# Layer 3 of a four-layer graph network: the edge products of a step at other places of a written-out order

## The chip, the cores and the metric

The kernel runs on one core of a Trainium2 chip. The metric is the time of one execution in microseconds (us), taken on the device. Three executions of the kernel before were timed, and a fourth was recorded by the hardware profiler.

## The reference, cut to what matters

Four graph layers work on 6250 nodes with 128 features and 100,000 edges sorted by destination. The change touches the fourth, "layer 3", alone: ten steps of a propagation (APPNP) over the graph with a self loop at every node.

```python
# K = 10, ALPHA = 0.1; src, dst with self loops added; norm = deg^-1/2[src] * deg^-1/2[dst]
def step(xk, _):
    msg = norm[:, None] * xk[src]
    agg = jax.ops.segment_sum(msg, dst, num_segments=n_nodes)
    return ((1.0 - ALPHA) * agg + ALPHA * h, None)
xK, _ = jax.lax.scan(step, x, None, length=K)
return jax.nn.relu(xK)
```

Each step needs all rows of the result of the step before: every node sums over the rows of its sources, which lie anywhere.

## The kernel before, in words

The 6250 nodes are 49 tiles of 128 (`NT`). The state `y` of a step is kept in SBUF as two float16 halves, in A in one step and in E in the next. A step makes the sums of the 49 destination tiles in two ways.

**Dense part.** The destination tiles 0 to 38 (`DENSE`) are multiplied with the adjacency matrix, which lies in DRAM as fp8 counts. Four tiles are a chunk; there are ten, 0 to 9, and chunk 9 has three tiles. A chunk takes 49 entries, one for each source tile, of two matmuls (the halves) with 512 columns, in chunk 9 with 384 columns (line 1988). The matrix comes in three pieces for each chunk, into a ring of four (line 764, SyncE's queue); a piece is loaded anew as soon as TensorE has used the one in its place, that is after the entries 16, 32 and 48 of a chunk.

**Edge part.** For the destination tiles 39 to 48 the rows of `y` are gathered by edge: 162 tiles of 128 edges, in 41 groups (0 to 40) of four tiles, the last of two. GpSimd issues one indirect DMA for each tile (line 1034) from the copy of `y` in DRAM (`table` in even steps, `x_spill` in odd ones), into a ring of five groups in the tile `arena`; TensorE multiplies them with one-hot matrices (line 2017), which VectorE makes (line 2874). The sums come out as three more chunks, numbers 10, 11 and 12, of four, four and two tiles (39 to 42, 43 to 46, 47 and 48), finished after the groups 17, 33 and 40.

**Chunk to state.** A finished chunk is copied out of PSUM by ScalarE ("copy", line 1476), transposed by TensorE ("turn", line 2001), and scaled and added by VectorE (line 2853 makes the part that doesn't depend on the sums, line 2888 adds). ScalarE makes the upper halves (line 1460) and VectorE the lower ones (line 2863). Then SyncE stores the chunk's rows to DRAM ("store", line 792). GpSimd begins the gathers of the next step when all 13 stores of this step have landed.

**Order.** The order of all this on TensorE, VectorE, ScalarE and SyncE is a list, `plan`, sorted by a place in units (lines 384 to 401). One dense entry of four tiles takes 2 units, one of three tiles 1.5; a step is 955 units long (`LONG`), and the dense entries of the next step follow at once. Every engine takes the entries in this order and waits at each on semaphores. Group g of the edge products stands at `first + EDGE_GAP * g`; the turn of a chunk 10 units behind its end (`TURN_LAG`) and its store 26 units behind (`STORE_LAG`). In the kernel before, the groups of a step stand at 84 + 22 g, so group 40 at 964, nine units into the next step; in the first step at 115 + 22 g. The order at a step's end is: chunk 9 ends (955), group 40 and chunk 12 end (964), turn 9 (965), turn 12 (974), store 9 (981), the load of a piece behind entry 16 of the next step (987), store 12 (990).

**Waits of the next step.** A dense entry of chunk 0 reads the source tile of its number from the new state. Before the entries that are keys of `READ_UPTO` TensorE waits until the lower halves of all tiles below the value are there:

```python
READ_UPTO = {0: 32, 32: 36, 36: NT - 1, NT - 1: NT}                       # line 413
if n > 0 and what == 0 and i in READ_UPTO:                                  # line 1985
    pe.wait_ge(sem("lower"), max(NT + tiles_done(step - 1, j) for j in range(READ_UPTO[i])))
```

Of the kernel before, what the change touches and what calls it, by code (L numbers as in the profile page):

```python
# [17 lines left out]
NT = (N_NODES + P - 1) // P  # L18
# [24 lines left out]
DENSE = NT - POOLED  # L43
# [2 lines left out]
ADJ_PITCH = 1 << 13  # L46
CHUNKS = (DENSE + CHUNK - 1) // CHUNK
POOL_CHUNKS = (POOLED + CHUNK - 1) // CHUNK
TURN_LAG, STORE_LAG, EDGE_LAG, EDGE_LATE, EDGE_GAP = 10, 26, 84, 115, 22
SCALE = 1024.0  # L50

BD, BK = 5, 26
# [37 lines left out]
def build(nc, t, out):  # L90
    ctx = ExitStack()
    with ctx:
# [23 lines left out]
        def sem(name):  # L116
            name = one_branch.get(name, name)
            if name not in names:
                names[name] = ctx.enter_context(nc.semaphore(name))
            return names[name]  # L120
# [227 lines left out]
        def chunk_nodes(c):  # L348
            if c < CHUNKS:
                return range(c * CHUNK, min((c + 1) * CHUNK, DENSE))  # L350
            return range(DENSE + (c - CHUNKS) * CHUNK, min(DENSE + (c - CHUNKS + 1) * CHUNK, NT))

        def chunk_at_cost(c):
            return 2 * NT * min(c * CHUNK, DENSE) // CHUNK
# [18 lines left out]
        def pooled_group(c):  # L373
            return (pooled_last[c - CHUNKS] - edge_first) // EG
# [10 lines left out]
        for step in range(STEPS):  # L385
            base = step * LONG
            for c in range(CHUNKS):
                for i in range(NT):
                    plan.append((base + chunk_at_cost(c) + 2 * i * len(chunk_nodes(c)) / CHUNK, 0, "dense", step, c, i))
                plan.append((base + chunk_at_cost(c + 1), -1, "copy", step, c, 0))  # L390
                plan.append((base + chunk_at_cost(c + 1) + TURN_LAG, 1, "turn", step, c, 0))
                plan.append((base + chunk_at_cost(c + 1) + STORE_LAG, 4, "store", step, c * CHUNK, chunk_nodes(c).stop))
            first = base + (EDGE_LAG if step else EDGE_LATE)
            for g in range(EGROUPS):
                plan.append((first + EDGE_GAP * g, 2, "edges", step, g, 0))
                plan.append((first + EDGE_GAP * g - 5 * EDGE_GAP // 2, 5, "hots", step, g, 0))
            for c in range(CHUNKS, CHUNKS + POOL_CHUNKS):
                plan.append((first + EDGE_GAP * pooled_group(c), 3, "copy", step, c, 0))
                plan.append((first + EDGE_GAP * pooled_group(c) + TURN_LAG, 1, "turn", step, c, 0))
                plan.append((first + EDGE_GAP * pooled_group(c) + STORE_LAG, 4, "store", step, chunk_nodes(c).start, chunk_nodes(c).stop))  # L400
# [9 lines left out]
        def tiles_done(step, i):  # L410
            return place[step, i] + 1

        READ_UPTO = {0: 32, 32: 36, 36: NT - 1, NT - 1: NT}

        assert edge_first >= 600
        taken, edges_in, done0, done_in = 0, {}, [], {}
# [62 lines left out]
        first = [("first", r) for r in range(PTN)]  # L479
# [1077 lines left out]
        def _(pe):  # L1557
# [363 lines left out]
            def after_l2(b):  # L1921
# [46 lines left out]
                if b == 0:  # L1968
# [4 lines left out]
                    for kind, step, what, i in plan:  # L1973
                        n = step * CHUNKS + what
                        if kind == "dense":
# [7 lines left out]
                            if n == 0 and i % T7 == 0:  # L1983
                                pe.wait_ge(sem("y_lower0"), i // T7 + 1)
                            if n > 0 and what == 0 and i in READ_UPTO:
                                pe.wait_ge(sem("lower"), max(NT + tiles_done(step - 1, j) for j in range(READ_UPTO[i])))
                            for h in range(2):
# [1095 lines left out]
```

## Time and profile before

| | us |
|---|---|
| median of 3 runs | 4969.4 (4966.07 to 4975.6) |
| the profiled execution's own time | 4971.43 |
| its span, from the first to the last instruction | 4969.5 |
| first and last dense matmul of layer 3 | 2686.7 and 4957.7 |
| mean granted TensorE clock | 0.915 |

The profile is one execution. Times are from the start of its span. For each group of instructions it has the busy time and the idle time of the engine before it, with what ended that idle time. "PE" is TensorE's matmul, "PEld" its weight load, "DVE" VectorE, "ACT" ScalarE, "POOL" GpSimd; "SPq" is SyncE's issue of a DMA. L1034 is line 1034 of the kernel.

Columns of the views: waits have who waited for whom, the total in us, the times and the longest. Windows have the stretch and its length, the busy us and count of PE, PEld, DVE, ACT and POOL, the granted TensorE clock as a share of full speed, the busy share of the DMA engines and GB/s; a step is taken from its first dense matmul to that of the next. A timeline has start, duration, the instruction, how many are merged (x), and in brackets the idle time before with what ended it. The chain has start, duration and what.

### The profile page before, as it was taken

To read this page: it belongs to the slowest core of one execution; us is meant where nothing else is said; L and a number is where in the kernel's file an instruction comes from. 1 tells how busy PE (TensorE), PEld (TensorE's weight loads), DVE (VectorE), ACT (ScalarE), POOL (GpSimd) and SP (SyncE) were. 2 spreads that over 40 slices of the span, in tenths; PEclk is the share of its full clock that TensorE was granted. 3 is DMA by queue.
4 is the path that set the end of the run, shared out by engine and by line. 5 is a ranking of instruction groups with operands and counts; after the bars stand their busy time and mean duration, and the time that the engine had idled before them with its cause. 6 is when DMAs were issued, how large, how long until landed. Compare 5 with 4: busy or idle time off the path is not lost.

```text
span 4969.5 us, 72321 instructions
## 1 busy us (share of the span) xinstructions
PE 4197.7 (84%) x25760; PEld 2695.7 (54%) x25760; DVE 2560.9 (52%) x8838; ACT 1034.5 (21%) x2922; POOL 3260.7 (66%) x3390
## 2 busy tenths in 40 slices
PE   3999588999985555667667999999999999999999
PEld 2776466766664555556554444444544444444444
DVE  7999545565554677778796222232232323222323
ACT  5887411111111001112224000000000000000101
POOL 2552377777775777777751767676766767676766
PEclk9999789999997667778778999999999999999999
DMA  5332322222222333333333666666666666666665
GB/s 150 113 111 97 86 66 70 71 66 70 71 70 70 94 96 95 96 95 95 88 78 105 204 190 204 198 202 201 205 199 199 204 196 208 196 203 198 202 200 165
DMA packets 455501, 686.46 MB, mean 138 GB/s; under 512 B 91793, under 2 KB 237879, under 8 KB 455120
## 3 DMA queue, kind: packets, MB, share of 16 engines
q1 hardware_dynamic: 341188, 454.71, 29.2%
q0 software_dynamic: 107584, 223.83, 17.2%
q8 instruction: 210, 3.44, 0.3%
q10 hardware_dynamic: 6364, 3.20, 0.2%
q14 instruction: 155, 1.27, 0.1%
HBM read 599.50 MB, written 82.31 MB: 137 GB/s over the span
## 4 chain that ended last, share of the span: by engine, by line
PE 31%; POOL 12%; DVE 6%; issue 5%; DMA 4%; ACT 1%; SPq 0%; POOLq 0%; DVEq 0%
PE ps L1988 26%; POOL arena L1034 10%; POOL E L999 2%; DVE B L2517 1%; DMA arena<-x_spill,src_i 1%; PE pt L2017 1%; DMA arena<-table,src_i 1%; PE ps L1810 1%; PE ps L2001 1%; PE pt L1827 1%; PE pt L1818 1%; DVE arena L2559 1%; DMA x_spill<-A 1%; DMA table<-E 0%; PE ps L1937 0%
## 5 line engine op out<-in xcount | busy, mean ns | idle before, releaser
L1988 PE MATMUL ps<-arena,E 128*128 128x512 fp8e4 (+1 forms) x4900 | 1080.6, 375 | 8.3 <-DVE C L2786 7.0
L1034 POOL DMA_INDIRECT arena<-table,src_i x810 | 782.0, 965 | 458.5 <-issue 233.6
L1988 PE MATMUL ps<-arena,A 128*128 128x512 fp8e4 (+1 forms) x4900 | 1078.9, 374 | 0.0
L1034 POOL DMA_INDIRECT arena<-x_spill,src_i x810 | 780.4, 963 | 348.6 <-issue 235.4
L984 POOL DMA_INDIRECT arena<-table,src_i x782 | 743.3, 950 | 346.9 <-issue 236.1
L999 POOL DMA_INDIRECT E<-gat_table,src_i x782 | 763.6, 976 | 269.8 <-issue 234.2
L1733 PE MATMUL ps<-E,arena 128*128 128x352 f32 (+22 forms) x2932 | 737.1, 403 | 118.4 <-DMA arena<-table,src_i 110.2
L1988 PEld LDWEIGHTS ps<-arena,E 128*128 128x128 f16 x4900 | 465.0, 98 | 507.3 <-issue 8.5
L1988 PEld LDWEIGHTS ps<-arena,A 128*128 128x128 f16 x4900 | 464.4, 98 | 495.7 <-issue 5.5
L2888 DVE SCALAR_TENSOR_TENSOR C<-ps,sc_b,scores 128x128 f32<-128x128 f32 x490 | 138.8, 345 | 1090.6 <-PE ps L2001 1089.0
L1733 PEld LDWEIGHTS ps<-E,arena 128*128 128x128 f32 x2932 | 491.2, 201 | 291.5 <-DMA arena<-table,src_i 141.0
L2437 DVE SCALAR_TENSOR_TENSOR E<-arena,pt 128x512 f32<-128x512 bf16 (+5 forms) x782 | 479.0, 675 | 24.5 <-PE ps L1733 23.7
L1810 PE MATMUL ps<-arena,B 128*128 128x144 f32 x2244 | 477.9, 364 | 0.0
L1810 PEld LDWEIGHTS ps<-arena,B 128*128 128x128 f32 x2244 | 391.4, 240 | 8.1 <-issue 5.9
L1476 ACT ACTIVATE O<-ps 128x512 f32<-128x512 f32 x100 | 58.7, 587 | 1527.9 <-PE ps L1988 1527.9
L1858 PE MATMUL pt<-ident,E 128*128 128x128 f32 x56 | 25.4, 454 | 354.6 <-ACT E L1268 354.6
L1069 POOL DMA_INDIRECT A<-first_rows,src_i x162 | 171.3, 1057 | 221.3 <-PE pt L2056 124.1
L1543 ACT ACTIVATE E<-ps 128x490 fp8e4<-128x490 f32 (+1 forms) x507 | 299.8, 596 | 61.6 <-PE ps L2072 57.6
L2081 PE MATMUL pt<-arena,E 128*128 128x258 f16 x1911 | 296.3, 275 | 1.4 <-ACT E L1543 1.3
L2874 DVE TENSOR_SCALAR rows<-w_gat,dst_f 128x54 f16<-128x54 bf16 (+17 forms) x966 | 159.3, 256 | 254.5 <-PE pt L2017 236.8
L2517 DVE TENSOR_SCALAR B<-w_gat,dst_f 128x256 f32<-128x256 bf16 x784 | 244.5, 381 | 0.0
L3002 DVE TENSOR_SCALAR O<-arena 128x245 bf16<-128x245 bf16 x1014 | 233.1, 293 | 4.1 <-PE ps L2072 4.0
(350 smaller groups left out, 4424.9 us busy)
## 6 DMA issues: line engine op xcount, KB each, us to landing
arena<-adj SPq DMA_DIRECT2D x180, 1024.0 KB
arena<-adj SPq DMA_DIRECT2D x90, 1088.0 KB
adj<-E SPq DMA_DIRECT2D x39, 784.0 KB, 3.7
arena<-table,src_i POOLq DMA_INDIRECT x1592
O<-dst_rows SPq DMA_DIRECT2D x112, 224.0 KB
arena<-adj SPq DMA_DIRECT2D x20, 768.0 KB
x_spill<-A SPq DMA_DIRECT2D x55, 256.0 KB, 2.5
arena<-x_spill,src_i POOLq DMA_INDIRECT x810
```

Source lines behind the costliest of these rows:

```text
L984: pool.indirect_dma_start(out=rows_ring[:, k % RING, :], out_offset=None, in_=table, in_offset=bass.IndirectOffsetOnAxis(ap=src_i[:, k:k + ...
L999: pool.indirect_dma_start(out=att_rows[:, b % 3 * AB + at, :], out_offset=None, in_=gat_table, in_offset=bass.IndirectOffsetOnAxis(ap=src_ ...
L1034: pool.indirect_dma_start(out=y_rows[:, g % ERING, k, :], out_offset=None, in_=(table, x_spill)[half], in_offset=bass.IndirectOffsetOnAxis ...
L1069: pool.indirect_dma_start(out=rows0[:, x % (2 * EG0), :], out_offset=None, in_=first_rows, in_offset=bass.IndirectOffsetOnAxis(ap=src_i[:, ...
L1543: act.activation(made[:, i % MADE, :, 2 * BD * q:2 * BD * q + w], ps[pair % 4][:, 0:w * NT].rearrange("p (d j) -> p j d", j=NT), ACT.Copy, ...
L1733: mm = pe.matmul(ps[m % 4][:, (lo - WD * m) * BASES:(hi - WD * m) * BASES], rows_ring[:, k % RING, :], m_ring[:, k % MS, lo - first_dst(k) ...
L1810: mm = pe.matmul(ps[i % 2][:, 0:WL2], edge_hot[:, (2 * b + half) % 3, k % AH, i % 2 * P:(i % 2 + 1) * P], weighted_rows[:, b % 2, k, :], s ...
L1988: mm = pe.matmul(chunk_banks[n % 2][:, 0:len(some) * P], y[:, i, h * D:(h + 1) * D], adj_ring[:, piece % ADJ_RING, 0:len(some), at:at + P] ...
L2081: mm = pe.matmul(bank0_of(m)[:, 0:2 * LO], made[:, m % MADE, j, :], y16[:, j, :], start=(j == 0), stop=(j == NT - 1))
L2437: dve.scalar_tensor_tensor(m_ring[:, k % MS, w, :], bc(iota_h[:, w], BASES), dst_rel[:, k:k + 1], row_bc(made_c[:, c % 2, at, :], w.stop - ...
L2517: a = dve.tensor_scalar(edge_hot[:, g % 3, k, :], iota_y, dst_f[:, g * AH + k:g * AH + k + 1], None, ALU.is_equal)
L3002: dve.tensor_scalar(hot_code[:, g % HOT, 0:BW], iota_w[:, 0:BW], slot_c[:, g // P, g % P:g % P + 1], None, ALU.is_equal).then_inc(sem("hot ...
```

## The change

The groups of a step stand at 110 + 21 g (group 40 at 950), in the first step at 145 + 21 g (group 40 at 985). Everything that hangs on them moves along: the one-hot matrices (`hots`), the copies, turns and stores of the chunks 10 to 12. The order at the end of a step other than the first becomes: group 40 and chunk 12 end (950), chunk 9 ends (955), turn 12 (960), turn 9 (965), store 12 (976), store 9 (981), the load behind entry 16 of the next step (987). In the first step it is: chunk 9 ends (955), turn 9 (965), store 9 (981), group 40 (985), load behind entry 16 (987), turn 12 (995), store 12 (1011), load behind entry 32 (1019). In the first step turn 10 comes behind turn 4; in the others the three pooled chunks keep their neighbours. `READ_UPTO` gets 39 in place of 48 for entry 36, 47 for entry 39 and 49 for entry 47 in place of 48.

```diff
-TURN_LAG, STORE_LAG, EDGE_LAG, EDGE_LATE, EDGE_GAP = 10, 26, 84, 115, 22
+TURN_LAG, STORE_LAG, EDGE_LAGS, EDGE_GAP = 10, 26, (145, 110), 21
...
-            first = base + (EDGE_LAG if step else EDGE_LATE)
+            first = base + EDGE_LAGS[min(step, len(EDGE_LAGS) - 1)]
             for g in range(EGROUPS):
                 plan.append((first + EDGE_GAP * g, 2, "edges", step, g, 0))
                 plan.append((first + EDGE_GAP * g - 5 * EDGE_GAP // 2, 5, "hots", step, g, 0))
...
-        READ_UPTO = {0: 32, 32: 36, 36: NT - 1, NT - 1: NT}
+        READ_UPTO = {0: 32, 32: 36, 36: DENSE, DENSE: NT - 2, NT - 2: NT}
```

## Rows read from the trace of the kernel before

**Rows 1.** Waits of TensorE in layer 3 (window 2680 to 4969)

```profile
PE pt L2017 <- DMA arena<-x_spill,src_i: 26.1, 20, 8.6
PE pt L2017 <- DMA arena<-table,src_i: 22.1, 14, 6.2
```

**Rows 2.** Windows of the steps 0, 1, 3 and 8

```profile
2686.65:2918.66 232.01, 224.56 (x1356) 110.37 (x1357) 78.71 (x371) 28.91 (x80) 155.56 (x162) 0.97 0.67 213
2918.66:3151.43 232.77, 223.54 (x1383) 110.88 (x1381) 66.15 (x337) 20.82 (x62) 155.51 (x162) 0.98 0.63 195
...
3377.37:3602.80 225.43, 221.09 (x1375) 109.96 (x1373) 65.61 (x337) 20.78 (x62) 156.62 (x162) 1.00 0.65 201
...
4506.29:4732.11 225.82, 221.41 (x1375) 109.79 (x1373) 65.89 (x337) 20.77 (x62) 156.72 (x162) 1.00 0.65 202
```

**Rows 3.** Waits of TensorE in step 1, then in step 3

```profile
PE pt L2017 <- DMA arena<-x_spill,src_i: 9.1, 2, 8.6
...
PE pt L2017 <- DMA arena<-x_spill,src_i: 4.3, 4, 2.0
```

**Rows 4.** Windows: TensorE directly behind the longest wait of step 1

```profile
2946.80:2951.20 4.40, 4.40 (x18) 1.69 (x19) 0.00 (x0) 0.00 (x0) 3.48 (x4) 0.50 0.24 62
```

**Rows 5.** Timeline of POOL: first gather of step 3, last of group 39

```profile
3391.93 0.94 POOL L1034 DMA_INDIRECT arena<-x_spill,src_i  x1 [20.96 <-DMA x_spill<-A]
...
3594.19 0.95 POOL L1034 DMA_INDIRECT arena<-x_spill,src_i  x1 [0.30 <-issue]
```

**Rows 6.** Timeline of PE: end of step 2, first groups of step 3

```profile
3379.53 0.26 PE L2017 MATMUL pt<-rel_i,arena 128*128 128x26 f16 x4
...
3382.11 0.38 PE L2001 MATMUL ps<-ident,O 128*128 128x128 f32 x2
...
3398.51 0.36 PE L2017 MATMUL pt<-weight_e,arena 128*128 128x2 f16 x8 [1.77 <-DMA arena<-x_spill,src_i]
...
3498.89 4.91 PE L1988 MATMUL ps<-arena,A 128*128 128x512 fp8e4 x22
3503.64 0.36 PE L2017 MATMUL pt<-weight_e,arena 128*128 128x44 f16 x8
```

**Rows 7.** Timeline of DVE: chunk 9 (x3), then chunk 12 (x2)

```profile
3380.66 0.87 DVE L2888 SCALAR_TENSOR_TENSOR C<-ps,sc_b,scores 128x128 f32<-128x128 f32 x3 [14.27 <-PE ps L2001]
3381.44 0.76 DVE L2863 SCALAR_TENSOR_TENSOR A<-C,A 128x128 f16<-128x128 f32 x3
...
3382.90 0.61 DVE L2888 SCALAR_TENSOR_TENSOR C<-ps,sc_b,scores 128x128 f32<-128x128 f32 x2 [0.17 <-DVE scores L2853]
3383.62 0.55 DVE L2863 SCALAR_TENSOR_TENSOR A<-C,A 128x128 f16<-128x128 f32 x2
```

**Rows 8.** Timeline of SP: the DMAs issued at the end of step 2

```profile
3377.56 0.36 SPq L764 DMA_DIRECT2D arena<-adj  x1
3382.22 0.36 SPq L792 DMA_DIRECT2D x_spill<-A  x1
3385.55 0.36 SPq L764 DMA_DIRECT2D arena<-adj  x1
3385.95 0.51 SPq L792 DMA_DIRECT2D x_spill<-A  x1
```

**Rows 9.** Line 792 in the window 3382 to 3383: one store, issue to landing

```profile
DMA to landing us min/median/max: 2.0/2.0/2.0
```

**Rows 10.** Line 792 in the window 2897 to 2898: one store, 2.9 us behind a load

```profile
DMA to landing us min/median/max: 2.8/2.8/2.8
```

**Rows 11.** The chain of waits in order of time (steps 2 and 3): start, us

```profile
3385.95 5.11 DMA x_spill<-A
...
3410.89 5.57 DMA arena<-x_spill,src_i
```

**Rows 12.** Timeline of POOL: end of the gathers of step 0, start of step 1

```profile
2914.82 0.95 POOL L1034 DMA_INDIRECT arena<-table,src_i  x1 [0.30 <-issue]
...
2940.43 0.95 POOL L1034 DMA_INDIRECT arena<-x_spill,src_i  x1 [22.16 <-DMA x_spill<-A]
```

## The prediction, made before the changed kernel was run

> **What bounds the kernel now.** I read three views in this order. The waits of TensorE in layer 3 name one cause worth a number: the edge products wait for gathered rows, 26.1 + 22.1 = 48.2 us in 34 waits [rows 1]. That is the most that the change can take away, beside what these waits do to the clock. The windows by step come next: a settled step lasts 225.4 us, and in step 3 TensorE waits 4.3 us of them [rows 2, 3], so its own work is 225.4 - 4.3 = 221.1 us a step. Steps 0 and 1 are longer, 232.0 and 232.8 us. In step 1 the waits are 9.1 us, and behind the longest the granted clock is 0.50, the lower of its two levels (1.2 GHz): 18 matmuls in 4.40 us [rows 4]. So step 1 loses 232.8 - 9.1 - 221.1 = 2.6 us more to the clock. The Trainium skill says of this (TensorE: Matmul & The Clock Gate, Part 1: The HAM clock gate) that throttled is the default and activity releases it; here the trace agrees (0.50 behind the wait, 1.00 over step 3), and the sum below doesn't rest on it.
>
> Then the timelines, for why these waits are there. GpSimd is idle 20.96 us between the last gather of a step and the first of the next, and a store to x_spill ends that [rows 5]. The rest of the time it issues 162 gathers back to back. So a step is a closed chain, which I add up from group 40 of step 2 at 3379.53 [rows 6]: to the first gather of step 3 at 3391.93, 12.40 us [rows 5]; to the first group's products at 3398.51, 6.58 us, where TensorE had waited 1.77 [rows 6]; and then 40 gaps of TensorE's own list to the next group 40, the rest of 225.4, that is 206.4. The chain runs through TensorE's sweep from group 0 to group 40. The gathers of groups 0 to 39 take 3594.19 + 0.95 - 3391.93 = 203.2 us [rows 5], 5.08 a group; TensorE's gap is 22 dense matmuls from 3498.89 to the next group at 3503.64, 4.75 us (0.216 each), and 0.2 for the group [rows 6]; that is 4.95, with the turns between some 5.1. Both go at the same pace, so TensorE stays just behind the rows all step long, and a late landing adds to its wait.
>
> **The change, part by part.**
>
> *Place of group 0.* It moves from unit 84 to 110 of a step, 26 x 0.216 = 5.6 us later. At 84 it stood at 19.4 us into the step (3398.51 - 1.77 - 3377.37) while its rows came at 21.1. Nothing is added or removed; the same 324 products are in the list.
>
> *Place of group 40 and the restart of the gathers.* This is the largest term. Before, group 40 to first gather was 12.40 us. Its parts: turn 12 at 3382.11, 2.58 behind group 40 [rows 6]; VectorE 0.79 later, done at 3384.17 [rows 7]; the store waits in SyncE's list behind the load that follows entry 16, which is issued at 3385.55, so it goes at 3385.95 [rows 8] and takes 5.11 us to land [rows 11]; 0.87 to the gather. In the new list, group 40 (950) is followed by three dense entries of chunk 9 (6 x 0.162 = 1.0 us; 0.162 is 0.216 x 384/512), three of the next step (6 x 0.216 = 1.3), then turn 12, so at 0.1 + 2.3 = 2.4. VectorE adds 0.79 + 1.27 (3382.90 to 3384.17) = 4.45 for chunk 12. Chunk 9's turn is done by then (five units later), and what is late next is VectorE: 1.0 us for the three prepared parts of chunk 9 (0.87 as for the other three-tile pass, and the 0.17 of idle time seen in rows 7), and 1.54 from its first addition to its last lower half (3380.66 to 3382.20) [rows 7]. Store 9 can go at 4.45 + 1.0 + 1.54 = 7.0. In SyncE's list it now stands ahead of the load behind entry 16, which TensorE reaches about 1.1 + 17 x 0.43 + 0.5 for two turns = 8.9. It follows the previous load, issued at 1.3 (0.2 behind the end of chunk 9, as 3377.56 is), by 5.7 us. Stores that follow a load by 4.66 us land in 2.0 [rows 8, 9], by 2.9 us in 2.8 [rows 10], by 0.4 us in 5.1 [rows 8, 11]. I take 2.0. Sum: 7.0 + 2.0 + 0.9 = 9.9 us from group 40 to the first gather, 2.5 less than before, although a second chunk is now in the chain.
>
> The Trainium skill (DMA: Bandwidth & Descriptors, Queues, rings and completion order) gives a reason: an engine takes its descriptors in ring order, and a semaphore increment lands only after every earlier write of that DMA engine, whatever the queue. The trace agrees, 5.1 against 2.0. The same page (Anatomy of one DMA) has a fixed 2.0 us plus bytes over 436 GB/s; by that estimate store 9 (192 KB) would take 2.4, and nine restarts would cost 4 us more than my sum.
>
> *Gap of 21.* TensorE's gap falls to 4.54 + 0.2, with turns 4.9 us, under the 5.08 of the gathers. So TensorE now gains 0.18 us a group on them. First gather at 9.9 - 1.1 = 8.8 us into the step (14.6 before), rows of group 0 there at 8.8 + 4.7 + 1.9 to 4.6 = 15.4 to 18.1 (landing behind the last issue: 1.9 for group 0 in rows 5 and 6, 5.57 - 0.95 = 4.6 in rows 11); group 0 is reached at 110 x 0.216 + 0.6 = 24.4. The lead is 6.3 to 9.0 us, and 39 x 0.18 = 7.0 of it is used up by group 39. So the waits at the start go, and small ones come at the last groups. The ring of five groups doesn't stop GpSimd: it wants group 5 at 8.8 + 25 = 34, and group 0 is used at 24.4; were that 9 us cover gone, the wait would be one for one in the chain.
>
> *The new chain of a step.* First gather to the end of group 39's, 203.2; its landing, between 1.9 and 4.6, and I take 4.3, since any of the last groups can be the late one; one gap to group 40, 4.75; restart 9.9. Together 222.15 us. With the ends of the landing it is 219.8 to 222.5, and TensorE's own work holds it to 221.1 at least. Before: 225.4.
>
> *First step.* Group 0 at 145 costs nothing: 30 units are 6.5 us, about what it waited for there. Then its gathers bound it: group 39's end at 2914.82 + 0.95 = 2915.8 [rows 12], + 4.3 + 4.75 gives group 40 at 2924.8. Turn 12 is 10 units behind (2.3), VectorE 0.79 + 1.27, the store 3.5 us behind a load, so 2.8 [rows 10], and 0.9: first gather of step 1 at 2932.8, against 2940.4 [rows 12].
>
> *READ_UPTO and the order of chunks.* No cost. Entry 36 stands 72 units, 15.6 us, into the step, and the last lower half is there at 7.0 - 1.1 = 5.9; in step 1 entry 47 (20.3 us) reads chunk 12, there at about 12. No wait of this kind shows before [rows 3], so finer pieces gain nothing either. If that cover of 9 us were gone, each us would count for one on TensorE, with the load queue behind it. The one-hot matrices move with their groups, and VectorE is busy 65.6 of 225 us [rows 2].
>
> *Sum.* Eight chains from step 1's first gather to step 9's: 2932.8 + 8 x 222.15 = 4710.0. Group 40 of step 9: + 203.2 + 4.3 + 4.75 = 4922.3, last dense matmul 1.1 later, 4923.4. Before it was at 4957.7. The tail behind it, 11.8 us, stays: the two chunks are then handled in the other order by the same instructions (within 0.5 us). So 34 us less: 4971.4 - 34 = 4937 for an execution like the profiled one. That one lies 2.0 us above the median of the runs shown, so 4935.
>
> **The rivals.**
>
> *TensorE at its floor* (gathers land early enough): 221.1 a step, 8 x 1.05 = 8 us less, 4927 beside the median. For it: landings of 1.9. Against: one late landing among the last few groups is enough.
>
> *The stores don't land faster* (by the skill's rule above this holds where the load ahead still writes after 5.7 us): restart 7.0 + 5.1 + 0.9 = 13.0, chain 225.25, and 2.3 more in step 0. 2.3 + 8 x 3.1 = 27 us given back: 4964, beside the median 4962. For it: chunk 9 now stands behind chunk 12 on VectorE, so that faster landing is all that pays for it. Against: the stores in rows 9 and 10.
>
> *Slower: the gathers' own pace.* Of the new chain 203.2 us are GpSimd's issues, and nothing on TensorE shortens them. VectorE's one-hot work now falls on other gathers than before; if that, or the denser traffic, draws the issues of 40 groups out by more than 34 / 8 = 4.3 us a step, 27 ns each, the change is a loss. At 6 us the chain is 228.2, 8 x 6 = 48 us above the forecast, 4983 beside the median. For it: GpSimd's busy time isn't even, 155.5 us in step 0 and 156.7 in step 8 [rows 2]. Against: that is 1.2 us apart, and between step 0 and step 3, where VectorE is busy 78.7 and 65.6 us, it is 1.1 with the other sign.
>
> **How the numbers follow.** Forecast 0.67, floor 0.14, stores not faster 0.12, slower pace 0.07. Each us in the restart or the landing is worth 8 to 9 us. The forecast's own range is 4925 to 4950; the range given, 4922 to 4962, takes in the floor and the stores that land no faster. About 0.2% (10 us) can be told from no change: faster 0.84 (the first two and a part of the third), same 0.09, slower 0.07.
>
> **What would show it.** Right: the first group of steps 1 to 9 no longer waits for a DMA, and short waits stand at groups 30 to 39; the idle time of GpSimd between steps is some 17 us in place of 21, and it is ended by a store that landed in about 2 us; the granted clock is 1.00 in step 1; a settled step lasts 222 us. Wrong: 5 us landings of that store, or steps at 225 us. Landings of the gathers that are longer than before in the last groups would make the size wrong, the mechanism not.

## The result

The changed kernel takes 4924.4 us, the median of four runs (4922.95 to 4933.52), against 4970.3 for the kernel before (four runs): 45.9 us less, a ratio of 0.9911 with a 95% interval of 0.9894 to 0.9928. The profiled execution took 4933.5 us, its span 4931.6.

What lies ahead of layer 3 moves from profile to profile (in two profiles of the changed kernel layer 3 begins at 2691.2 and at 2686.7 us), so I size everything below by the length of layer 3, from its first to its last dense matmul. It is 2271.0 us before (2686.7 to 4957.7) and 2229.1 after (2691.2 to 4920.3): 41.9 us less. In a second profile of the changed kernel, taken with the experiments, layer 3 begins at 2686.7 as before and ends at 4913.8: 2227.1 us, 43.9 less. The forecast was 34. Two profiles of one kernel thus differ by 2.0 us in layer 3; smaller differences than that tell nothing below.

**Windows by step of the changed kernel**, steps 0, 1, 3 and 5, in the columns of [rows 2]:

```profile
2691.21:2924.43 233.22, 224.87 (x1356) 109.31 (x1357) 79.03 (x371) 28.89 (x80) 156.56 (x162) 0.98 0.67 212
2924.43:3151.88 227.45, 222.04 (x1387) 109.86 (x1385) 65.42 (x336) 21.20 (x63) 155.99 (x162) 1.00 0.64 200
...
3373.55:3593.94 220.39, 220.39 (x1374) 110.28 (x1373) 65.60 (x337) 20.78 (x62) 154.40 (x162) 1.00 0.66 206
...
3814.33:4036.48 222.15, 220.89 (x1376) 110.01 (x1373) 65.20 (x337) 20.78 (x62) 156.49 (x162) 1.00 0.65 204
```

Step 1 has lost 5.3 us and its clock is full (0.98 before). A settled step (2 to 8) is 220.4 to 222.2 us long where it was 225.4 to 226.6, and in step 3 TensorE is busy all the time: 220.39 of 220.39. Step 0 gained nothing.

**The waits of TensorE in layer 3 of the changed kernel** (total, times, longest), against [rows 1]:

```profile
PE pt L2017 <- DMA arena<-table,src_i: 8.5, 9, 2.3
PE pt L2017 <- DMA arena<-x_spill,src_i: 7.4, 9, 2.0
```

48.2 us have become 15.9, and 11.5 of them lie in the steps 0 and 1. These 32.3 us are not all of the gain: TensorE is also busy 10 us less, and its granted clock over layer 3 is 1.00 in place of 0.99. Layer 3 before, then changed:

```profile
2686.65:4957.69 2271.04, 2221.17 (x13721) 1100.78 (x13722) 673.17 (x3405) 218.06 (x638) 1562.35 (x1620) 0.99 0.64 200
2691.21:4920.35 2229.14, 2211.09 (x13725) 1100.67 (x13726) 669.47 (x3404) 218.42 (x639) 1553.85 (x1620) 1.00 0.65 204
```

**The end of step 2 of the changed kernel** on SP, PE, DVE and POOL, the same stretch as in [rows 5] to [rows 8] (start, us, instruction, idle before):

```profile
3373.74 0.36 SPq L764 DMA_DIRECT2D arena<-adj  x1
3376.67 2.72 SPq L792 DMA_DIRECT2D x_spill<-A  x2
3381.63 0.36 SPq L764 DMA_DIRECT2D arena<-adj  x1
```

```profile
3372.47 0.26 PE L2017 MATMUL pt<-rel_i,arena 128*128 128x26 f16 x4
...
3374.84 0.38 PE L2001 MATMUL ps<-ident,O 128*128 128x128 f32 x2
...
3398.70 0.35 PE L2017 MATMUL pt<-weight_e,arena 128*128 128x2 f16 x8
```

```profile
3375.36 0.61 DVE L2888 SCALAR_TENSOR_TENSOR C<-ps,sc_b,scores 128x128 f32<-128x128 f32 x2 [14.18 <-PE ps L2001]
3376.09 0.55 DVE L2863 SCALAR_TENSOR_TENSOR A<-C,A 128x128 f16<-128x128 f32 x2
3376.56 0.87 DVE L2853 SCALAR_TENSOR_TENSOR scores<-C,sc_a,B 128x128 f32<-128x128 f32 x3
3377.47 0.87 DVE L2888 SCALAR_TENSOR_TENSOR C<-ps,sc_b,scores 128x128 f32<-128x128 f32 x3
3378.25 0.75 DVE L2863 SCALAR_TENSOR_TENSOR A<-C,A 128x128 f16<-128x128 f32 x3
```

```profile
3364.07 0.94 POOL L1034 DMA_INDIRECT arena<-table,src_i  x1 [0.30 <-issue]
3381.93 0.94 POOL L1034 DMA_INDIRECT arena<-x_spill,src_i  x1 [16.92 <-DMA x_spill<-A]
...
3581.97 0.95 POOL L1034 DMA_INDIRECT arena<-x_spill,src_i  x1 [0.30 <-issue]
```

Read it as one chain. Group 40 is at 3372.47; turn 12 is 2.4 us behind it; VectorE ends chunk 12 at 3376.64 and chunk 9 at 3379.00, 6.5 behind group 40. The two stores go at 3376.67 and as soon as chunk 9 is done, 2.9 and some 5.3 us behind the last load; the next load follows at 3381.63. The first gather is at 3381.93, 2.9 us behind the second store's issue: 9.46 us behind group 40, where it was 12.40. GpSimd's idle time between steps is 16.92 us in place of 20.96. The first group of step 3 (3398.70) waits for nothing.

### The profile page after: what moved, and what is told of

Same layout as the page of the kernel before. It is cut to its first block, busy times and chain, and to the rows that moved or that the text cites. A ratio compares the mean times of both kernels' runs of the same rounds, so it can differ in the third digit from the quotient of the medians.

```text
span 4931.6 us, 72321 instructions
## 1 busy us (share of the span) xinstructions
PE 4191.0 (85%) x25760; PEld 2696.4 (55%) x25760; DVE 2556.1 (52%) x8838; ACT 1034.5 (21%) x2922; POOL 3253.1 (66%) x3390
## 4 chain that ended last, share of the span: by engine, by line
PE 40%; POOL 12%; DVE 6%; issue 5%; DMA 2%; ACT 1%; POOLq 0%; DVEq 0%
PE ps L1988 33%; POOL E L999 7%; POOL arena L1034 6%; PE ps L1810 2%; DVE B L2517 2%; PE pt L2017 1%; PE ps L2001 1%; DVE arena L2559 1%; DMA arena<-table,src_i 1%; PE pt L1818 1%; PE pt L1827 1%; DMA arena<-x_spill,src_i 1%; DMA E<-gat_table,src_i 0%; PE ps L1937 0%; DVE arena L2540 0%
## 5 line engine op out<-in xcount | busy, mean ns | idle before, releaser
L999 POOL DMA_INDIRECT E<-gat_table,src_i x782 | 765.5, 979 | 269.1 <-issue 235.5
```

What stands on the lines that cost most here:

```text
L999: pool.indirect_dma_start(out=att_rows[:, b % 3 * AB + at, :], out_offset=None, in_=gat_table, in_offset=bass.IndirectOffsetOnAxis(ap=src_ ...
```

## The experiments

In the table every row is one profile. "Restart" is the time from group 40 to the first gather of the next step in a settled step, "step" the length of the steps 2 to 8. No profile of the kernel before was taken beside the experiments. In the comparison of b_store22, a_store34, b_gap21 and b_finer the last, which turns out to change nothing, can stand for it: 2269.3 us against 2271.0.

| kernel | layer 3, us | restart | step | whole time against the kernel before beside it |
|---|---|---|---|---|
| before | 2271.0 | 12.4 to 12.8 | 225.4 to 226.6 | |
| changed | 2229.1, 2227.1 | 9.5 (once 11.1) | 220.4 to 222.2 | 0.9911 (0.9894 to 0.9928), 0.9915 (0.9901 to 0.9929) |
| b_store22 | 2227.5 | 7.3 (once 8.2) | 220.7 to 221.4 | 0.9905 (0.9878 to 0.9931) |
| a_store34 | 2285.5 | 15.8 to 16.1 | 226.1 to 228.2 | 1.0050 (1.0028 to 1.0072) |
| b_gap21 | 2282.4 | 14.5 (once 15.2) | 225.9 to 229.0 | 1.0014 (0.9993 to 1.0035) |
| b_finer | 2269.3 | 12.3 to 12.9 | 225.2 to 226.2 | 0.9999 (0.9981 to 1.0018) |
| a_gap22_2 | 2222.5 | 6.8 | 220.4 | 0.9901 (0.9886 to 0.9916) |
| a_first115_2 | 2229.2 | 9.5 | 220.4 to 221.6 | 0.9909 (0.9894 to 0.9924) |
| c_110_22_2 | 2216.2 | 6.8 | 220.4 | 0.9889 (0.9874 to 0.9904) |

**The stores four units earlier, nothing else: b_store22.** This moves the stores of all chunks; the gathers wait for the last one, that of chunk 12. On the kernel before:

```diff
-TURN_LAG, STORE_LAG, EDGE_LAG, EDGE_LATE, EDGE_GAP = 10, 26, 84, 115, 22
+TURN_LAG, STORE_LAG, EDGE_LAG, EDGE_LATE, EDGE_GAP = 10, 22, 84, 115, 22
```

> The kernel before with STORE_LAG 22 in place of 26, nothing else. Store 12 then stands at 986 of the list, ahead of the load that follows entry 16 (987). Theory (a step is a closed chain: gathers, last groups, turn, store, its landing, first gather): the store goes when VectorE is done, 4.7 us behind group 40, lands in 2.0 and not 5.1 us, and the gathers restart 7.6 us behind group 40 in place of 12.4. The chain of a step falls from 225.4 to 220.6, so TensorE's own work, about 221.1 us, bounds it: 4928 to 4938 us in all, although no group is moved. GpSimd idles some 16 us between steps. Rival (the places and the gap of the groups make the gain, the store is hidden anyway): within 5 us of the kernel before, 4970.

Measured: 4956.4 us against 5002.5 beside it, layer 3 2227.5 us. SP, group 40 on PE and the first gather on POOL at the end of a step, then TensorE's waits in layer 3:

```profile
3421.51 0.36 SPq L764 DMA_DIRECT2D arena<-adj  x1
3426.17 2.33 SPq L792 DMA_DIRECT2D x_spill<-A  x2
3429.50 0.36 SPq L764 DMA_DIRECT2D arena<-adj  x1
```

```profile
3423.48 0.26 PE L2017 MATMUL pt<-rel_i,arena 128*128 128x26 f16 x4
...
3430.82 1.43 POOL L1034 DMA_INDIRECT arena<-x_spill,src_i  x1 [15.74 <-DMA x_spill<-A]
```

```profile
PE pt L2017 <- DMA arena<-table,src_i: 7.6, 4, 6.3
PE pt L2017 <- DMA arena<-x_spill,src_i: 5.6, 7, 3.1
```

Both stores now go before the load (3429.50), and the gathers restart 7.3 us behind group 40 (7.6 was worked out). The restart has lost 5.1 us. For 1.75 of them SyncE no longer waits for its turn behind the load: the store of chunk 12 goes 4.67 us behind group 40, where it went 6.42 behind. The other 3.3 us lie between the store's issue and the first gather: 2.67 in place of 5.98. No group has moved, and layer 3 is as short as with the whole change. This is the finding of the study: the position of the last store against one load in SyncE's list is worth the 43 us. The absolute time lay outside what I had expected (4928 to 4938), since the kernel before took 5002 there; the ratio is what I expected.

**The same store behind the load, in the changed kernel: a_store34.**

```diff
-TURN_LAG, STORE_LAG, EDGE_LAGS, EDGE_GAP = 10, 26, (145, 110), 21
+TURN_LAG, STORE_LAG, EDGE_LAGS, EDGE_GAP = 10, 34, (145, 110), 21
```

> The changed kernel with STORE_LAG 34 in place of 26: groups, gap and waits as changed, but store 9 at 989, behind the load after entry 16, and store 12 of the first step behind the load after entry 32. Theory: restart 9.3 + 5.1 + 0.9 = 15.3 us behind group 40 in place of 9.5, a step of about 227 us in place of 221.2, 4970 to 4980 us in all: the whole gain gone. Rival (the places make the gain): as the changed kernel, 4924.

Measured: 5035.4 us against 5002.5, layer 3 2285.5 us, 56.4 above the changed kernel and 14.5 above the kernel before. SP and POOL (group 40 is at 3435.90), then the waits:

```profile
3440.09 0.36 SPq L792 DMA_DIRECT2D x_spill<-A  x1
3445.05 0.36 SPq L764 DMA_DIRECT2D arena<-adj  x1
3445.45 0.51 SPq L792 DMA_DIRECT2D x_spill<-A  x1
```

```profile
3451.97 0.94 POOL L1034 DMA_INDIRECT arena<-x_spill,src_i  x1 [23.63 <-DMA x_spill<-A]
```

```profile
PE pt L2017 <- DMA arena<-x_spill,src_i: 32.5, 36, 4.1
PE pt L2017 <- DMA arena<-table,src_i: 27.2, 35, 2.1
```

Store 9 goes 0.4 us behind the load, and the first gather is 6.5 us behind the store's issue, in place of 2.9. Restart 16.1 here, 15.9 in most steps (15.3 worked out), and a step of 226.1 to 228.2 us (227). All the places of the change, without the early store, are worse than the kernel before. The whole time, 0.5% up, lies above what I had expected (4970 to 4980, 0 to 0.2% up). Layer 3 explains 14.5 us of it. The rest lies ahead of layer 3, which the edit doesn't touch: layer 3 begins at 2742.8 us here and at 2722.0 in b_finer. What makes that difference isn't shown.

**The smaller gap alone: b_gap21**, on the kernel before:

```diff
-TURN_LAG, STORE_LAG, EDGE_LAG, EDGE_LATE, EDGE_GAP = 10, 26, 84, 115, 22
+TURN_LAG, STORE_LAG, EDGE_LAG, EDGE_LATE, EDGE_GAP = 10, 26, 84, 115, 21
```

> The kernel before with a gap of 21 alone, groups at 84 + 21 g, group 40 at 924. The restart hangs on store 9 then, which keeps its place at 981; it lies 41 units + 2.2 + 2.9 us, 14.4 us, behind group 40. Theory: chain 203.2 + 4.3 + 4.75 + 14.4 = 226.7 us a step, waits of TensorE at the last groups, 4972 to 4982 us. Rival (a smaller gap pays by itself, since the gathers are ahead at a step's end): 4950 or less.

Measured: 5006.7 against 5002.5, within what can be told, and layer 3 11.4 us longer, 2282.4. The waits in layer 3:

```profile
PE pt L2017 <- DMA arena<-table,src_i: 32.4, 31, 6.7
PE pt L2017 <- DMA arena<-x_spill,src_i: 23.1, 28, 2.4
```

There are 59 waits in place of 34: TensorE's list runs ahead of the gathers and pays in small pieces. The restart is 14.5 us (group 40 at 3389.36, first gather at 3403.83; 14.4 worked out), since chunk 9's store is the last one; its turn now lies 41 units behind group 40, and the store 57. So this run has two things in it, the smaller gap and a restart 2.1 us longer, and the 11.4 us are not the price of the gap alone. The steps, 225.9 to 229.0 us, lie about the 226.7 worked out; the whole time was not told apart from no change.

**The finer waits alone: b_finer**, the new `READ_UPTO` on the kernel before:

```diff
-        READ_UPTO = {0: 32, 32: 36, 36: NT - 1, NT - 1: NT}
+        READ_UPTO = {0: 32, 32: 36, 36: DENSE, DENSE: NT - 2, NT - 2: NT}
```

> The kernel before with the new READ_UPTO alone. Theory: no wait of a dense matmul on lower halves shows in either trace, the last lower half is there some 9 us before the entry that reads it: no change, 4970 within 4 us. Rival (the coarse wait cost something at entry 36): up to 1 us a step, 4960.

Measured: 5003.9 against 5002.5, layer 3 2269.3 (2271.0 before). It makes no difference. The waits are near those of the kernel before (28 for 34):

```profile
PE pt L2017 <- DMA arena<-x_spill,src_i: 21.9, 14, 8.3
PE pt L2017 <- DMA arena<-table,src_i: 21.2, 14, 6.4
```

**Four runs that can't size anything: after_again, a_first115, a_gap22, c_110_22.** The changed kernel again, and three edits of it that follow below.

> The changed kernel again, on the chip of the three runs beside it. Theory: the gain of the change lies in layer 3 alone, from 2271 to about 2229 us from its first to its last dense matmul; what lies ahead of it differs from execution to execution and doesn't belong to the change. So layer 3 is 2227 to 2232 us here, whatever the whole time. Rival (the earlier layers, or the chip, make part of the difference): layer 3 off by more than 5 us.

> The changed kernel with the first step at 115 + 21 g in place of 145 + 21 g. Theory: the gathers of step 0 start when the stores ahead of it have landed, so group 39 of step 0 is no earlier; the waiting moves from its last groups to its first, and the gathers of step 1 start within 2 us of before: layer 3 within 3 us of the changed kernel's. Rival (the place in the first step is worth the wait it takes away): 6 us more.

> The changed kernel with a gap of 22 in place of 21: group 40 at 990, store 12 the last, ahead of the load after entry 32. Theory: restart 8.2 us or less behind group 40, steps at TensorE's own 221 us with no waits for rows in steps 2 to 9; step 0 shorter by 5, step 1 longer by 6, since its gathers start later: layer 3 2224 to 2231 us. Rival (the gap of 21 is needed): 5 us or more above the changed kernel.

> All steps at 110 + 22 g with STORE_LAG 22: as the run with gap 22, but the first step earlier by 35 units, so that its last store, and with it the gathers of step 1, come 7 us earlier. Theory: some 2 us of waiting at the first group of step 0, at most 2 in step 1, none after: layer 3 2216 to 2224 us, 5 to 13 us under the changed kernel. Rival (gathers bound steps 0 and 1 anyway): layer 3 as the changed kernel's, 2229.

They ran on a chip on which the kernel before takes 6259.9 us. Ratios: 0.9943 (0.9920 to 0.9965), 0.9971 (0.9950 to 0.9992), 0.9911 (0.9887 to 0.9936) and 0.9914 (0.9891 to 0.9936). Layer 3 is 2742.6, 2740.5, 2730.4 and 2722.1 us there, so my expectation of 2227 to 2232 "whatever the whole time" failed, and so did the lengths expected of the others. Layer 3 of the changed kernel there, and what TensorE waited for in it:

```profile
3438.57:6181.16 2742.59, 2372.78 (x13724) 1133.03 (x13725) 671.23 (x3404) 217.86 (x639) 1548.67 (x1620) 0.93 0.54 166
```

```profile
PE ps L2001 <- ACT O L1476: 155.3, 28, 13.1
PE ps L1988 <- issue: 122.0, 185, 2.0
PE pt L2017 <- issue: 54.8, 70, 2.6
```

Against the first profile of the changed kernel (2229.14 us, of which TensorE is busy 2211.09), 352 us more are idle time and 162 us more are busy time, at a granted clock of 0.93 in place of 1.00. Much of the idle time has no releaser ("issue"), which the first profile does not show before a matmul at all. The median duration of a dense matmul is the same in both (379 ns), and so is nearly that of a gather (944 and 947 ns). What held the engines between their instructions I haven't shown. The 426 us that the expectation of after_2 names count TensorE's matmuls (122.0) and its weight loads (304.3) together, and its 14 us are weight loads alone. The four runs were repeated on another chip.

**The changed kernel again: after_2.**

> The changed kernel again. The last four runs fell on a chip on which the kernel before takes 6260 us; there the engines stand idle between instructions with no wait in the profile (426 us before the dense matmuls, 14 in the first profile), so they don't size a term of 1% and are repeated here. Theory: layer 3, first to last dense matmul, 2227 to 2232 us whatever the whole time, against 2271 for the kernel before. Rival: off by more than 5 us.

Measured: 4930.7 against 4974.7 beside it, layer 3 2227.1 us, as expected. In one restart of its eight settled ones, that of step 2, the first gather came 4.5 us behind the last store's issue in place of 2.9, though the store went 5.3 us behind the load as in the others; why isn't shown.

**The first step: a_first115_2.**

```diff
-TURN_LAG, STORE_LAG, EDGE_LAGS, EDGE_GAP = 10, 26, (145, 110), 21
+TURN_LAG, STORE_LAG, EDGE_LAGS, EDGE_GAP = 10, 26, (115, 110), 21
```

> The changed kernel with the first step at 115 + 21 g. Theory: the wait of 6 us at group 0 of step 0 comes back, those at its last groups go, the gathers of step 1 start within 2 us: layer 3 within 3 us of the changed kernel's. Rival: 6 us more.

Measured: 4930.8 against 4974.7, layer 3 2229.2 us. Step 0 is 240.6 us and step 1 221.9, together 462.5, against 231.8 + 227.3 = 459.1 for the changed kernel beside it. So the place in the first step moves the waiting from one step to the next. Layer 3 is 2.1 us longer than in after_2 and 0.1 longer than in the first profile of the changed kernel: if the place is worth anything, it can't be told from the 2.0 us between these two.

**The gap at 22: a_gap22_2**, and **all steps at 110 + 22 g with the store at 22: c_110_22_2.**

```diff
-TURN_LAG, STORE_LAG, EDGE_LAGS, EDGE_GAP = 10, 26, (145, 110), 21
+TURN_LAG, STORE_LAG, EDGE_LAGS, EDGE_GAP = 10, 26, (145, 110), 22    # a_gap22_2
+TURN_LAG, STORE_LAG, EDGE_LAGS, EDGE_GAP = 10, 22, (110, 110), 22    # c_110_22_2
```

> The changed kernel with a gap of 22. Theory: no waits for rows in steps 2 to 9, step 0 shorter and step 1 longer by about 6 us: layer 3 2224 to 2231 us. Rival (the gap of 21 is needed): 2234 or more.

> All steps at 110 + 22 g with STORE_LAG 22. Theory: gathers restart some 8 us behind group 40 and TensorE sets every step from 2 on, 221 us; steps 0 and 1 lose 2 us each at most: layer 3 2216 to 2224 us, the best of all. Rival: gathers bound steps 0 and 1 anyway, layer 3 2229.

Measured: 4924.5 and 4919.1 against 4974.7; layer 3 2222.5 and 2216.2 us. In a_gap22_2 step 0 is short (224.1) and step 1 pays for it (235.5, with one wait of 11.0 us): 7.7 less and 8.2 more than in after_2, where some 6 was expected of each. Its layer 3 lies 1.5 us under the range expected, 2224 to 2231. c_110_22_2 pays in step 0 alone; windows of its steps 0, 1, 3 and 9:

```profile
2686.44:2919.28 232.84, 224.55 (x1356) 110.37 (x1357) 78.53 (x371) 29.00 (x80) 155.95 (x162) 0.97 0.68 212
2919.28:3139.67 220.39, 220.39 (x1375) 110.26 (x1373) 65.74 (x337) 20.81 (x62) 155.45 (x162) 1.00 0.66 206
3360.06:3580.46 220.40, 220.40 (x1376) 110.24 (x1374) 65.58 (x337) 20.77 (x62) 155.44 (x162) 1.00 0.66 206
4682.41:4902.64 220.23, 220.23 (x1375) 110.17 (x1372) 66.25 (x338) 22.89 (x62) 155.40 (x162) 1.00 0.62 191
```

From step 1 on a step is 220.4 us and TensorE never waits for a row; the one wait for rows left in layer 3 is 7.0 us at the first group of step 0. It is the fastest of all, 11.6 us under the changed kernel in the same comparison (4930.7), 0.24%. The intervals of the ratios overlap (0.9874 to 0.9904 and 0.9901 to 0.9929), but no execution of the one lies among those of the other (4916.1 to 4920.9, and 4926.9 to 4937.6), and the two layer-3 lengths, 2216.2 and 2227.1, differ by the same 11 us. In both kernels with a gap of 22 the restart is 6.8 us; the last store goes 4.3 us behind a load.

## Why the prediction was right, and where its size was off

- *The bound.* Right: the waits for rows were the price, 48.2 us, and 32.3 of them went. The clock's part in step 1 went with them. TensorE's busy time fell by 10.1 us in layer 3, where the prediction names 2.6, in step 1.
- *The closed chain.* Right, and shown from both sides: four edits moved the restart to 7.3, 9.5, 14.5 and 15.9 us, worked out beforehand as 7.6, 9.9, 14.4 and 15.3, and layer 3 followed: 2227.5, 2229.1, 2282.4, 2285.5. Under some 9.5 us it gives little more (steps of 220.4 us with 6.8), since TensorE's own work is the bound there. What the prediction did not see is that the early store does it alone. It had the later places and the smaller gap as parts of the gain, and b_store22 has neither.
- *The restart as the largest term.* Right in each part: turn 12 at 2.4, chunk 12 done at 4.2 (4.45), chunk 9 at 6.5 (7.0), 2.9 from the store's issue to the gather, as taken. VectorE took the prepared parts of chunk 9 without the pause I had added. The 2.4 us that the prediction works out for store 9 from the Trainium skill (DMA: Bandwidth & Descriptors, Anatomy of one DMA) rest on a fit that the page gives for DMAs issued from GpSimd, and SyncE issues this store; it landed 2.05 or 2.06 us behind its issue at the end of the steps 1, 3, 5 and 7, and the measurement decides.
- *Gap of 21.* Half right. The lead at group 0 was there, and small waits stand at the last groups: in step 2 and in the steps 5 to 8, 210 to 216 us into the step. In step 1 they begin 90 us into it, long before group 30. But a gap that outruns the gathers is no gain. In a_gap22_2, the changed kernel with 22, no wait for rows is left from step 2 on, and its layer 3 is 4.6 us shorter than that of after_2.
- *First step.* Right in its sum, in part by luck. The first gather of step 1 was worked out 246.1 us behind the first dense matmul and came at 246.0 in after_2 and 247.6 in the first profile. In after_2 group 40 came 1.1 us later than worked out, and the restart, 6.8 us in place of 8.0, was as much shorter.
- *READ_UPTO at nothing.* Right, b_finer.
- *The sum.* 34 us was too little; the mis-sized term is the chain of a settled step, 222.15 us. From step 2's first gather to step 9's it is 7 x 222.15 = 1555.1 us, and in after_2 it is 1546.3, 8.8 less; the end of step 9 is another 1.5. Two sizes were too long. I took the gathers of groups 0 to 39 at 203.2 us from one step of the kernel before (its steps have 201.5 to 204.5), and in step 3 of the changed one they take 3581.97 + 0.95 - 3381.93 = 201.0, in other settled steps up to 203.1. And I took TensorE's own work for 221.1 us, which held the floor too high: it is 220.39 in the steps without a wait. Where the 0.7 us of the kernel before come from isn't shown; the granted clock in its step 3 is 1.00. So the chain was mostly not the bound. In step 5 it was, and there the sum held: 203.1 for the gathers and a step of 222.15.
- *The rival that came nearer.* *TensorE at its floor*, given 0.14, is nearer to what happened than the forecast: 4927 against 4924.4 measured, and the forecast's own range began at 4925. I had argued that one late landing is enough against it; late landings came, in step 2 and in the steps 5 to 8, at 0.4 to 1.3 us a step, and TensorE's floor took up the rest. Of the 45.9 us in the medians only 41.9 to 43.9 lie in layer 3; the rest lies in layers that the change doesn't touch.
- *A count.* A step has 344 edge products in the trace, not 324; nothing hangs on it.
- *The stores that land no faster* fell: 2.9 us from issue to gather against 6.0. *Slower by the gathers' pace* fell: GpSimd was busy 154.4 us in step 3 and not more than 156.6 in any step shown.

## What to carry to other kernels

Close the loop first: when a step needs the last row of the step before, add up the chain from one group to the same group a step later, and look at its shortest links, the stores and what stands ahead of them in their queue. A small store that the next step waits for belongs ahead of a large prefetch in the same queue; 4 units of a hand-written order, under 1 us of TensorE's time, gave the whole 43 us here. And spread the consumer no tighter than the producer delivers: a gap of 22 beat 21 by 4.6 us in the changed kernel.

## What the runs showed of the hardware

- A store issued 0.4 us behind a load of 1 MB (some are 1088 KB) on the same queue let the next gather start 5.9 to 6.4 us after its issue when it had 128 KB (kernel before, b_finer: up to 6.5) and 6.2 to 6.5 us when it had 192 KB (a_store34). Issued 6.6 us behind the load, 128 KB took 2.7 us, once 3.5 (b_store22); issued 5.3 us behind it, 192 KB took 2.9 us, once 4.5. The load costs the store some 3.2 to 3.8 us. No run tells whether the order in the queue does this or the sharing of the DMA engines: no store was moved to another queue.
- On one chip the same kernels ran 26% longer at the same median instruction durations. In layer 3 of the changed kernel 352 of the 513 us more were idle time of TensorE, and 162 us busy time at a granted clock of 0.93 in place of 1.00. An absolute time worked out from one chip's profile did not hold on another (4970, 4975, 5002 and 6260 us for the kernel before in four comparisons). Ratios held better, and even they shrank (0.9943 for the changed kernel).
- With no wait left the steps are equal: steps 1 to 8 of c_110_22_2 are 220.39 or 220.40 us each.
